# A graph layer's third and fourth gathered rows: one buffer and an adding transfer, or two buffers and an addition on GpSimd

## The reference

```python
edge_index = jnp.stack([src, dst])
x = x + _L0_gnn_ref(_layernorm(x, axis=-1), edge_index, L0_gnn_W, L0_gnn_b)
x = x + _L0_ffn_ref(_layernorm(x, axis=-1)[None], L0_ffn_base_W, ...)[0]
```

## Time and profile before

| | us |
|---|---|
| median of three runs | 2184.49 |
| the profiled execution | 2184.77 |
| its span | 2182.9 |
| stage one, to the last product | about 950 |
| stage two with PE at its steady pace | 1020 to the end |

### The profile page before, as it was taken

One profiled execution on the slowest core, in us unless ns is written; L12 is line 12 of the kernel. 1 busy time (PEld: TensorE's weight loads), 2 busy tenths in 40 slices (PEclk: granted clock), 3 DMA queues, 4 the chain that ended last, 5 costly groups with the idle time before them and its releaser, 6 DMA issues.

```text
span 2182.9 us, 33549 instructions
## 1 busy us (share of the span) xinstructions
PE 2129.1 (98%) x11577; PEld 1966.5 (90%) x11577; DVE 1537.7 (70%) x3709; ACT 522.6 (24%) x888; POOL 633.3 (29%) x773
## 2 busy tenths in 40 slices
PE   7999999999999999949999999999999999999999
PEld 6888888888888888838999999999999999999999
DVE  7877667666666455537777777777777777777774
ACT  4333232232332333411112111111121121111211
POOL 2200000000000430025443544444445444444430
PEclk9999999999999999978999999999999999999999
DMA  5533334333333344456556556556565565565540
GB/s 215 193 126 145 135 126 145 129 132 137 128 141 135 126 144 174 158 174 150 163 150 160 157 150 167 158 149 165 152 159 157 146 171 154 148 166 152 159 125 39
DMA packets 107463, 325.23 MB, mean 149 GB/s; under 512 B 28576, under 2 KB 28912, under 8 KB 107206
## 3 DMA queue, kind: packets, MB, share of 16 engines
q1 hardware_dynamic: 60550, 221.02, 28.6%
q0 software_dynamic: 46784, 102.75, 20.4%
HBM read 261.20 MB, written 125.49 MB: 177 GB/s over the span
## 4 chain that ended last, share of the span: by engine, by line
PE 92%; DVE 4%; issue 2%; POOL 1%; DMA 1%; ACT 0%; DVEq 0%; POOLq 0%; ACTq 0%
PE bo L664 27%; PE bo L666 27%; PE bo L665 27%; PE bt L672 6%; PE bo L787 2%; PE bo L791 2%; PE bo L789 2%; DVE acc L1036 1%; DVE acc L1044 1%; DVE st L1046 0%; PE bt L781 0%; DVE z_lo L1115 0%; POOL g L556 0%; DMA g<-h_rows,row_now 0%; DVE acc L1071 0%
## 5 line engine op out<-in xcount | busy, mean ns | idle before, releaser
L664 PE MATMUL bo<-base_hi,z_hi 128*128 128x380 f32 (+1 forms) x1896 | 654.7, 345 | 5.1 <-issue 5.1
L665 PE MATMUL bo<-base_lo,z_hi 128*128 128x380 f32 (+1 forms) x1896 | 639.2, 337 | 0.0
L666 PE MATMUL bo<-base_hi,z_lo 128*128 128x380 f32 (+1 forms) x1896 | 639.0, 337 | 0.0
L664 PE MATMUL bo<-w_hi,u_hi 128*128 128x512 f32 x1264 | 500.3, 396 | 3.9 <-issue 3.2
L666 PE MATMUL bo<-w_hi,u_lo 128*128 128x512 f32 x1264 | 493.5, 390 | 0.0
L665 PE MATMUL bo<-w_lo,u_hi 128*128 128x512 f32 x1264 | 492.8, 390 | 0.0
L664 PEld LDWEIGHTS bo<-base_hi,z_hi 128*128 128x128 f32 x1896 | 358.8, 189 | 5.5 <-issue 5.5
L665 PEld LDWEIGHTS bo<-base_lo,z_hi 128*128 128x128 f32 x1896 | 359.0, 189 | 0.0
L666 PEld LDWEIGHTS bo<-base_hi,z_lo 128*128 128x128 f32 x1896 | 357.5, 189 | 0.0
L556 POOL DMA_INDIRECT g<-h_rows,row_now x237 | 307.5, 1297 | 91.2 <-issue 91.2
L664 PEld LDWEIGHTS bo<-w_hi,u_hi 128*128 128x128 f32 x1264 | 238.1, 188 | 51.7 <-issue 4.1
(11 more groups left out here) (127 smaller groups left out, 2391.9 us busy)
## 6 DMA issues: line engine op xcount, KB each, us to landing
xn<-x SPq DMA_DIRECT2D x79, 512.0 KB, 3.5
r_rows<-xn SPq DMA_DIRECT2D x79, 512.0 KB
acc<-r_rows SPq DMA_DIRECT2D x79, 512.0 KB, 4.3
out<-acc SPq DMA_DIRECT2D x79, 512.0 KB, 4.8
h_rows<-hrow SPq DMA_DIRECT2D x78, 512.0 KB, 2.6
g<-h_rows,row_now POOLq DMA_INDIRECT x316, 6.2
base_raw<-base_t SPq DMA_DIRECT2D x8, 571.0 KB, 4.5
w_raw<-w_t SPq DMA_DIRECT2D x8, 512.0 KB, 7.4
```

Of the source, the lines that this page charges most:

```text
L664: nc.tensor.matmul(ps, hi[:, k, :], m_hi[:, k, n], start=(k == 0), stop=False)
L665: nc.tensor.matmul(ps, hi[:, k, :], m_lo[:, k, n], start=False, stop=False)
L666: return nc.tensor.matmul(ps, lo[:, k, :], m_hi[:, k, n], start=False, stop=(ends and k == KB - 1))
```

## The change

The fourth gather no longer adds in memory. It goes to a buffer of its own, `g[q][3]`, and is issued right behind the third edge's, ahead of the first two edges'. The two count up one semaphore, `g_rest_in`. Where POOL issued the adding gather it now waits for both and adds `g[q][3]` to `g[q][2]` itself, 1024 float32 in each of 128 partitions (L538 of the changed kernel). DVE waits for that addition in place of the transfer. SP's hold at the start of stage two now covers all four gathers of tile 0. There are two more buffers of 4 KiB in each partition. The arithmetic of DVE, ACT and PE is the same.

```diff
@@ -258,7 +258,7 @@
         z = [sb(f"z{q}", [P, D], F32) for q in range(2)]
         z_hi = [sb(f"z_hi{q}", [P, KB, P], F32R) for q in range(2)]
         z_lo = [sb(f"z_lo{q}", [P, KB, P], F32R) for q in range(2)]
-        g = [[sb(f"g{q}{r}", [P, D], F32) for r in range(SKIPPED + 1)] for q in range(2)]
+        g = [[sb(f"g{q}{r}", [P, D], F32) for r in range(ROUNDS)] for q in range(2)]
         here = at[0]
         at[0] = w_at + DEEP * 4 * D
         xg = sb("xg", [P, D], F32)
@@ -289,8 +289,8 @@
         r_stored, zero_stored = sem("r_stored"), sem("zero_stored")
         slots_set, slots_put, slots_in = sem("slots_set"), sem("slots_put"), sem("slots_in")
         r_in = [sem(f"r_in{q}") for q in range(DEEP)]
-        g_in = [[sem(f"g_in{q}{r}") for r in range(SKIPPED + 1)] for q in range(2)]
-        g_full = [sem(f"g_full{q}") for q in range(2)]
+        g_in = [[sem(f"g_in{q}{r}") for r in range(SKIPPED)] for q in range(2)]
+        g_rest_in, g_full = [sem(f"g_rest_in{q}") for q in range(2)], sem("g_full")
         out_stored = [sem(f"out_stored{q}") for q in range(DEEP)]
 
         consts, zeroed, ident_ok, half_ok = (sem("consts"), sem("zeroed"), sem("ident_ok"),
@@ -411,8 +411,9 @@
                 if s.has(5):
                     a = s.mod(5, DEEP)
                     if s.has(4) and not s.has(3):
-                        for r in range(SKIPPED + 1):
+                        for r in range(SKIPPED):
                             sp.wait_ge(g_in[0][r], 16)
+                        sp.wait_ge(g_rest_in[0], 16 * (ROUNDS - SKIPPED))
                     if s.has(-1):
                         sp.wait_ge(out_stored[a], 16 * (s.uses(5, DEEP) - 1))
                     sp.dma_start(acc[a][:], r_dram[rows(s.tile(5)), :]).then_inc(r_in[a], 16)
@@ -533,13 +534,9 @@
             def step(s):
                 if s.has(3):
                     q = s.mod(3, 2)
-                    pool.wait_ge(g_in[q][SKIPPED], 16 * s.uses(3, 2))
-                    carry_wait(4 + 4 * (s.q % 2))
-                    nc.gpsimd.indirect_dma_start(
-                        g[q][SKIPPED][:], None, h_dram,
-                        bass.IndirectOffsetOnAxis(ap=row_now[q][:, ROUNDS - 1:ROUNDS], axis=0),
-                        bounds_check=NPAD + P - 1, oob_is_err=True, compute_op=ALU.add) \
-                        .then_inc(g_full[q], 16)
+                    pool.wait_ge(g_rest_in[q], 16 * (ROUNDS - SKIPPED) * s.uses(3, 2))
+                    nc.gpsimd.tensor_tensor(g[q][SKIPPED][:], g[q][SKIPPED][:],
+                                            g[q][SKIPPED + 1][:], ALU.add).then_inc(g_full, 1)
                 if s.has(2):
                     pool.wait_ge(acc_stats_ok, s.tile(2) + 1)
                     nc.gpsimd.tensor_tensor(pw[:], pin[:], neg_half[:, 0:1], ALU.pow) \
@@ -551,13 +548,14 @@
                         copy_slots(t, q)
                     pool.wait_ge(row_copied, t + 1)
                     carry_wait(5 + 4 * (s.q % 2))
-                    for r in (SKIPPED, 0, 1):
+                    for r in (SKIPPED, SKIPPED + 1, 0, 1):
                         skips = r < SKIPPED
                         nc.gpsimd.indirect_dma_start(
                             g[q][r][:], None, h_dram,
                             bass.IndirectOffsetOnAxis(ap=row_now[q][:, r:r + 1], axis=0),
                             bounds_check=(NPAD if skips else NPAD + P) - 1,
-                            oob_is_err=not skips).then_inc(g_in[q][r], 16)
+                            oob_is_err=not skips) \
+                            .then_inc(g_in[q][r] if skips else g_rest_in[q], 16)
 
             pipeline(pool, step, -4, TILES - 3, 5)
 
@@ -1040,7 +1038,7 @@
                 n = s.tile(3)
                 q = s.mod(3, 2)
                 a = acc[s.mod(3, DEEP)]
-                dve.wait_ge(g_full[q], 16 * s.uses(3, 2))
+                dve.wait_ge(g_full, n + 1)
                 accs.link(dve, nc.vector.tensor_tensor(a[:], a[:], g[q][SKIPPED][:], ALU.add))
                 for h in range(2):
                     accs.link(dve, nc.vector.bn_stats(st[:, h, :], a[:, h * HALF:(h + 1) * HALF]))
```

## The result

The changed kernel takes 2289.05 us (median of four runs, 2286.42 to 2294.35) against 2184.44 us before: ratio 1.0483, 95% interval 1.046 to 1.0505, 104.6 us slower. The forecast was 2213.5 us. The direction and the range held; the change was 3.6 times as large as forecast (104.6 us against 29).

What follows compares the result with a forecast made beforehand. PE was taken to bound the kernel, busy 98% of the span, at 15.0 us a tile. 2184.5 + 29 (additions delaying L1059 over 74 tiles) + 0 (passage) = 2213.5 us; range 2181 to 2330.

Steps and rivals of the forecast that it cites:

- the slack of 0.25 us: DVE's chain from the router's first operation to L1138: any delay above 0.25 us a tile comes out of PE.
- The removed gather, the moved gather, the bytes: POOL's gathers in stage two: dropping the adding gather and issuing the fourth second gain or lose nothing; no byte added.
- The sign of being wrong: Profile check: L1059 should follow the addition's end by under 0.2 us; wrong if L1059 or L1095 starts during it.
- Whom it holds up: POOL's reading addition makes DVE operations with two SBUF inputs wait; L1059 starts 0.41 us late.
- the row of the rival: Evidence for no hold-up: DVE's L849 took its usual 1.28 us inside a 12.36 us POOL operation.
- When it starts, and where the chain is then: Stage-two tile: addition starts at 1509.9 to 1511.1, taken as 1510.6, after L1095 ended at 1510.58 and before L1059.
- the forecast's kind: Tiles where the addition delays L1059: 15.39 us against 15.0, 0.39 us each, 29 us in all; chance 0.42.
- the second rival: Addition starts before L1095 and stops DVE's router chain: 2.0 us a tile, 147 us in all, 2332; chance 0.21.
- The free window: DVE's gap between L1095's end and L1059, 2.06 us, said to be less than the addition.
- The passage: Between the stages: up to 10.2 us gained from DVE's waits, 7.2 us lost before `pw`; taken as 0.
- The no-hold-up rival: POOL's reads don't stop DVE in stage two; tile stays 15.0 us, 2184.5 within 4 us; chance 0.30.
- the faster rival: The passage gains from the fourth gather's earlier landing and stage two loses nothing: -8, 2176.5; chance 0.07.

Runs made afterwards that it cites:

- experiment 4: Changed kernel's gathers without POOL's addition; DVE adds the third and fourth edges' rows itself, one more 1.22 us operation a tile: 2269.44 us, ratio 1.0384.
- experiment 1: Changed kernel, but POOL adds only the first 128 of 1024 columns: 2189.57 us, ratio 1.0019.
- Experiment 2: Changed kernel with POOL's addition replaced by a memset of 2560 columns, which reads nothing: 2238.2 us, ratio 1.0245.
- experiment 7: Changed kernel with DVE adding for tiles 0 to 2, and POOL's later additions behind `pw` (2183.83 us) or waiting for DVE's L1042 of the tile before (2182.93 us).
- the gated addition: Changed kernel, POOL's whole addition waiting for DVE's L1042 of the tile before, so it lies beside the statistics: 2195.24 us, ratio 1.0046.
- experiment 5 (half): Changed kernel, but POOL adds only 512 of the 1024 columns: 2213.61 us, ratio 1.0125.
- experiment 6 (behind `pw`): Changed kernel with `pw` moved ahead of the whole addition in POOL's step: 2198.71 us, ratio 1.0061.
- experiment 3: Kernel before the change, adding gather kept, plus a 1024-column POOL addition each tile that nobody waits for: 2458.08 us, ratio 1.1239.
- the double one: Changed kernel with one more 1024-column POOL addition ahead of the one that counts, into an unread buffer: 2395.69 us, ratio 1.0907.

## Why the prediction was right and where it was wrong

*What bounds the kernel; the slack of 0.25 us.* Right. Everything that held DVE's chain up came out at PE's L785, and experiment 4's 1.22 us made 15.9 us tiles.

*The removed gather, the moved gather, the bytes.* Right: 102.75 MB again, and with a short addition (experiment 1) the steady tile loses 0.07 us.

*The sign of being wrong.* The prediction called itself wrong if L1059 or L1095 started while the addition ran. They do start, in 55 and 7 tiles, and are held inside their own records; the sign had to be the end and not the start.

*The addition's length.* Right: 2.40 us against 2.4. The estimate of 2.25 us worked out from the Trainium skill's figure in "GPSIMD Engine Reference" (section "Performance versus the Vector engine") was a little low.

*Whom it holds up.* The mechanism was right: addition and DVE operation exclude each other, L1057 ends with the addition, and the row of the rival (a long POOL operation on 75 elements) did not carry over to 1024. What I added to the forecast's checks was wrong: I looked for idle time in front of L1057, and there is none, since the wait is inside its duration. And I counted only operations with two SBUF inputs as candidates: L1100, which has one, is held as well. The Trainium skill, in "SBUF — State Buffer" (section "Who interferes with whom"), has both: a GpSimd instruction that only writes leaves a DVE instruction with two SBUF inputs alone, and a `tensor_scalar` that runs in a two-port mode contends with GpSimd without that exception. Experiment 2 agrees with the first half (47 of 47 not held) and fits the second (16 of 16 held), though no run shows in which mode L1101 ran; I had read only the half about two inputs.

*When it starts, and where the chain is then. This is the step that failed.* The prediction "put the last byte at 1509.6 to 1510.6" and took a start of 1510.6, 9.4 us behind the statistics. Measured were 9.4 to 11.9 us, 10.1 on average. The rows themselves land at 10.0, with or without additions (experiment 4). In the tile from 1515.64 the ebb of the earlier trace rows is gone:

```profile
1523.00:1524.00 1.00, 1.00 (x8) 1.00 (x7) 0.86 (x5) 0.86 (x2) 0.09 (x1) 1.00 1.02 406
1524.00:1525.00 1.00, 1.00 (x8) 1.00 (x7) 0.83 (x7) 0.00 (x0) 0.00 (x0) 1.00 0.88 304
```

By 1524.0, 8.4 us behind the statistics, 1.56 MB had moved, which is what the prediction wanted to have through; yet the addition started at 1525.33. The first two edges' rows and the load of `r_rows` (issued at 1523.94) were under way too, and the prediction's sum of bytes left them out. No experiment separates them, so why the rows land at 10.0 stays open.

- In the 55 tiles of the forecast's kind, the loop is 10.11 us to the addition's start, 2.40 us, and 3.42 us from its end to the next statistics: 15.92 us as measured, not 15.39. They lose 0.88 us each, 48 us in all, not 0.39. This part follows from the 0.7 us.
- The other 17 tiles lose 2.8 us each, 47 us in all, and this part does not follow from a late start. Their additions met the router's chain, as the second rival had it, which I gave 0.21 as a case of its own, with every tile or none. Five were early starts (1.8 us each, 9 us). Twelve were additions at 9.4 to 10.7 us that met a late chain: five at the turn of the loop of six tiles (2.6 us each, 13 us; before the change that tile took 15.6 to 15.8 us and the next 14.7), seven behind a stretch at half clock (3.5 us each, 25 us). The prediction took the chain's place from one tile. It named the clock only as something that might be added to the second rival; by experiment 4's 1.55 us the seven stretches alone are an estimate of 11 us, and the rest of the 25 is the hold.
- The free window was not 2.06 us either. L1100 (the old L1102, 1511.01 in the tile of the prediction) was left out of the chain and is held like the rest. An addition from 1510.6 would have been running when L1102 wanted to start, so the prediction's own start would have cost every tile about what it cost the five early ones, 1.8 us and not 0.4 (an estimate from those five). That most tiles came out as the forecast's kind is luck: the rows landed late enough to miss L1100.
- My loss of 0.41 us was the small difference of a late start and a length, 2.4 us against that window. An error of 0.7 us in the start, small beside 15, was larger than the term. 48 + 47 = 95 us is what was measured for the steady tiles. The stated range held only because it reached into the second rival's case; the forecast's own case ended at 2260.

*The passage.* I took 0 between -10 and +7, and it cost 6.5 us. The gain was there (DVE waited 10.2 us for adding transfers before, and experiments 4 and 7 shorten PE's wait from 28.3 to 22.5 us), though little of it arrives: tile 4's statistics end no earlier in experiment 4 and 1.3 us earlier with the gate in experiment 7. Three additions on POOL, each in front of `pw` and the next gathers, more than took it back: DVE's wait for `pw` is 12.0 us.

*The no-hold-up rival* (0.30) and *the faster rival* (0.07) fell by the same rows; the latter's mechanism is what experiment 7 gets.

## What to carry to other kernels

Time on an idle engine is free only if what it does beside the busy one does not exclude it: list the neighbour's operations that start inside the new one, by form, before calling it hidden. Here the same 2.40 us cost 95 us in the steady tiles beside the scale and the router and next to nothing beside the statistics; one semaphore moved it. When a start or the edge that it must miss scatters, count the tiles on each side instead of forecasting one tile, ask whether longer tiles cost clock as well, and look for a hold-up in the mean duration of a short operation, not in the idle column.

## What the runs showed of the hardware that I had not expected

- A memset on POOL (2.23 us, 2560 columns) holds DVE's `TENSOR_SCALAR` on 128 x 6 up (for example 2.04 us instead of 0.23) but no operation with two SBUF inputs. A `TENSOR_SCALAR` on 128 x 1 (L1047, L1096) was held by neither: 74 times beside the gated addition, never.
- A hold ends a little before the addition's record does. In experiment 5 (half) nine L1058 that started in the last 0.15 us of it kept their 0.15 us, and the 24 that started earlier were held; in experiment 6 (behind `pw`) L1034 kept its 1.28 us 64 times of 64.
- PE had half its clock (1.2 GHz) for stretches of 3.4 us in the kernels whose tiles got long: seven in the changed kernel, 35 in experiment 3, 30 in the double one, none in the steady stretch of the kernel before and of experiments 1, 6 and 7. One stretch cost 1.55 us (experiment 4).
- Not held by an addition, in all kernels here: reductions, reciprocals, batch-norm statistics, and operations with an input in PSUM.
- POOL's addition of 1024, 512 and 128 columns takes 2.40, 1.29 and 0.46 us, which is about 0.19 us and 2.17 ns a column (1.11 us for the second 512); in a row of eight, 128 columns take 0.57 us each.
- An addition right behind a gather's issue held DVE 0.7 us before its own record begins (3.61 us in all for a 0.23 us operation). What holds in that time is open.
